# First weight blocks loaded one stage early, store waits moved to the stages that read the data, and a reordered gather stage in a graph-transformer kernel

## What is computed

```
xn = layernorm(x)
x  = x + graph_net(xn, edges) + linear_attention(xn)       # graph_net: x1 = xn @ W1 + b1, then 4 hops
x  = x + mixture_of_experts(layernorm(x))                  # 8 experts, top 2
xn = layernorm(x)
x  = x + (xn @ W.T + bias) + relu_linear_attention(xn)     # W: 1024x1024, scattered from 20000 edge weights
x  = x + gated_mlp(layernorm(x))                           # int32 weights, hidden 384
```

## The kernel before

| tag | function | work |
|---|---|---|
| gs | graph_sort | sorts the edges into buckets (the scatter of the sorted slots runs beside em and m0, on POOL) |
| em | embed | layernorm, x1 = xn @ W1 |
| m (first) | attention, called m0 | q, k, v for 8 head pairs, softly mapped |
| o (first) | project_and_count, o0 | output projection, and the counts and weights of the graph by one-hot products |
| gb, gl | graph_overflow, graph_layer | the 4 hops |
| ro, ex | route, experts | router and scatter to seats; 27 tiles of expert work |
| se | serve | gathers the experts' rows, adds them, layernorm, product with the scattered W |
| m (second) | attention, m1 | as m0, with relu |
| o (second) | project, o1 | output projection, layernorm |
| ff | gated_mlp | last stage |

## Time and profile before

### The profile page before, as it was taken

The page is one execution under the profiler, slowest core; times in us unless marked ns, Lnnn a source line. Parts: engine busy times, 40 slices in busy tenths (PEclk is TensorE's granted clock), DMA queues, the critical chain, the costliest instruction groups (busy, mean ns, idle before and its releaser), DMA issues. The chain is left out here.

```text
span 2633.7 us, 33722 instructions
## 1 busy us (share of the span) xinstructions
PE 2250.2 (85%) x12654; PEld 1997.2 (76%) x12654; DVE 1629.6 (62%) x2675; ACT 1018.6 (39%) x1616; POOL 252.4 (10%) x259
## 2 busy tenths in 40 slices
PE   1689999996994999944499999985979999979798
PEld 1669999995783877744388888874769999978697
DVE  8865555665875788844499999976733333335422
ACT  1512222223863454411488888862111221221120
POOL 0357760000000000002000000002100000000000
PEclk9899999998996999955699999997989999989899
DMA  0251211113442000056545544315421111133314
GB/s 15 83 175 38 66 39 37 42 43 120 131 130 68 9 9 9 20 200 220 199 173 203 183 161 163 142 49 211 159 73 37 52 57 37 48 114 127 119 44 132
DMA packets 104211, 259.04 MB, mean 98 GB/s; under 512 B 17103, under 2 KB 44102, under 8 KB 104046
## 3 DMA queue, kind: packets, MB, share of 16 engines
q1 hardware_dynamic: 93230, 235.88, 25.7%
q0 software_dynamic: 10816, 20.99, 2.8%
HBM read 291.69 MB, written 84.49 MB: 143 GB/s over the span
## 5 line engine op out<-in xcount | busy, mean ns | idle before, releaser
L2050 DVE TENSOR_TENSOR ex_wl<-ex_raw,ex_wh 128x1024 fp32r<-128x1024 f32 x324 | 375.7, 1219 | 58.2 <-ACT ex_wh L2117 57.5
L2117 ACT ACTIVATE ex_wh<-ex_raw 128x1024 fp32r<-128x1024 f32 x324 | 328.8, 1057 | 92.7 <-DMA ex_raw<-in_experts 58.0
L1362 DVE TENSOR_TENSOR m_kvf<-m_bank,m_bkv 128x256 f32<-128x256 f32 (+1 forms) x160 | 67.9, 424 | 232.0 <-PE m_bank L1267 216.1
L1031 POOL DMA_INDIRECT scratch_slots<-pay,idx x160 | 198.4, 1240 | 59.8 <-issue 59.8
L1267 PE MATMUL m_bank<-m_w_lo,xh 128*128 128x256 f32 (+1 forms) x1280 | 178.3, 281 | 0.0
L1267 PE MATMUL m_bank<-m_w_hi,xl 128*128 128x256 f32 (+1 forms) x1280 | 177.4, 280 | 0.2 <-issue 0.2
L1267 PE MATMUL m_bank<-m_w_hi,xh 128*128 128x256 f32 (+1 forms) x1280 | 177.5, 281 | 0.1
L1523 PE MATMUL gl_bank<-gl_gh,gl_al 125*125 125x512 f32 x400 | 158.9, 397 | 8.7 <-DVE gl_al L1691 8.7
L1267 PEld LDWEIGHTS m_bank<-m_w_lo,xh 128*128 128x128 f32 (+1 forms) x1280 | 163.9, 186 | 0.1
L1267 PEld LDWEIGHTS m_bank<-m_w_hi,xl 128*128 128x128 f32 (+1 forms) x1280 | 162.4, 186 | 0.6 <-issue 0.6
L1267 PEld LDWEIGHTS m_bank<-m_w_hi,xh 128*128 128x128 f32 (+1 forms) x1280 | 161.4, 186 | 0.6 <-issue 0.6
(11 more groups left out here) (407 smaller groups left out, 5241.3 us busy)
## 6 DMA issues: line engine op xcount, KB each, us to landing
ex_raw<-in_experts SPq DMA_DIRECT2D x324, 512.0 KB
m_w_raw<-in_qkv SPq DMA_DIRECT2D x48, 512.0 KB
ex_xr<-scratch_seats SPq DMA_DIRECT2D x27, 512.0 KB, 3.7
scratch_served<-ex_y SPq DMA_DIRECT2D x27, 512.0 KB, 2.6
scratch_at<-m_ats SPq DMA_DIRECT2D x48, 209.0 KB, 1.9
o_ar<-scratch_at SPq DMA_DIRECT2D x18, 512.0 KB
o_xr<-scratch_res SPq DMA_DIRECT2D x18, 512.0 KB
scratch_res<-o_xr SPq DMA_DIRECT2D x18, 512.0 KB
```

What stands on the lines that cost most here:

```text
L1031: e.indirect_dma_start(dram["slot_rows"], bass.IndirectOffsetOnAxis(idx[:, k:k + 1].bitcast(U32), 0), pay[:, k, :], None).then_inc(scat.se ...
L1362: e.tensor_tensor(f, bank[KVB + s % 3][0:r, 0:W2], bkv[0:r], ALU.add)
L2050: return e.tensor_tensor(wl[:, n % RING], raw[:, unit[1]], wh[:, n % RING].bitcast(F32), ALU.subtract)
L2117: e.activation(wh[:, n % RING], raw[:, unit[1]], ACT.Copy).then_inc(high.sem)
```

## The change

1. Two buffers now live over all stages: `raw` (four weight slots of 128x1024) and `xr` (three chunks of 128x1024; attention's output staging `ats` is a view of it). `Ahead` loads the first weight units of the next stage into `raw` while the present one still runs: 8 small units in gs for em; 3 in em for m0; 4 in m0 for o0; 4 in ex (at its tile 13) for se; 3 in se for m1; 4 in m1 for o1; 2 in o1 for ff. SP waits, where needed, for the last `make_low` that reads a slot. o1's ring shrinks from 6 slots to 4. Semaphores of such loads are handed on to the next stage.
2. The waits for `res` stores at the end of o0, ro, se and o1, for `at` stores at the end of m0 and m1, and for the `x2` stores at the end of gl are gone; SP of the stage that reads the data waits for them ahead of its loads. em and ex keep theirs.
3. gl's last update is handed to SP chunk by chunk instead of all five at once.
4. o0, se and o1 have new orders on ACT and DVE, below all `serve`: the Sqrt table is loaded at once by a dummy (`warm`), the Sqrt of the first chunk and `scale(0)` come before weight units 2 to 7, `mix(1)` between them, PE turns chunk 1 after the product of chunk 0 instead of within it, the third gather goes ahead of POOL's bias addition.

```diff
+class Ahead:
+    def __init__(self, p, raw, units):
+        self.raw, self.units = raw, units
+        self.loaded = [p.raises(f"ahead{s}", [u], 16) for s, u in enumerate(units)]
+
+    def load(self, e, w_dram, s):
+        e.dma_start(self.raw[:, s], w_dram[self.units[s]]).then_inc(self.loaded[s].sem, 16)
...
 class Resident:
...
     def make_high(self, e, u):
         s = u % self.slots
-        e.wait_ge(*self.loaded[s][u])
+        e.wait_ge(*(self.ahead.loaded if u < self.slots else self.loaded)[s][u])
```

attention, SP at its end:

```diff
+            for s in (3, 0, 1, 2):
+                if s < 3:
+                    e.wait_ge(*low[s][PAIRS - 1])
+                ahead.load(e, then, s)
             store(PAIRS - 1)
-            for t in range(NT):
-                e.wait_ge(*stored[t][PAIRS - 1])
```

project, SP:

```diff
+            for t in at_stored:
+                e.wait_ge(*t.last())
             load_at(0)
-            for u in range(SLOTS):
-                w.load(e, w_dram, u)
             load_at(1)
+            for t in base_stored:
+                e.wait_ge(*t.last())
...
+                if c == 1:
+                    e.wait_ge(*w.low[KC - 1])
+                    for s in range(2):
+                        ahead.load(e, then, s)
```

project, ACT (DVE likewise with make_low, and o0 similarly):

```diff
+            w.make_high(e, 0)
+            w.make_high(e, 1)
             split_at(0)
-            for u in U:
+            for u in range(2, KC):
                 w.make_high(e, u)
```

graph_layer, the end of DVE and of SP:

```diff
-            update(1, range(HALF)).then_inc(last_out.sem)
+            for d in range(HALF):
+                update(1, [d]).then_inc(last_out.sem)
...
+            for c in T[HALF:]:
+                e.wait_ge(*last_out[c])
+                move(e, dram["x2"][nodes(c)], g[:, c], stored[c].sem)
```

experts, SP:

```diff
+                if s == NTILE // 2:
+                    for t in range(4):
+                        ahead.load(e, then, t)
```

serve, ACT:

```diff
+            e.activation(warm[:], share[:, 0, 0:1], ACT.Sqrt)
             w.make_high(e, 0)
             w.make_high(e, 1)
             weigh(0)
-            for u in range(2, 4):
-                w.make_high(e, u)
+            w.make_high(e, 2)
+            w.make_high(e, 3)
+            n.root(e, 0)
+            w.make_high(e, 4)
+            w.make_high(e, 5)
             split(0)
-            for u in range(4, KC):
-                w.make_high(e, u)
+            w.make_high(e, 6)
+            w.make_high(e, 7)
             weigh(1)
```

## The result

The changed kernel takes 2587.0 us (median, 2584.3 to 2587.9) beside 2621.9 for the kernel before: ratio 0.9868, with a 95% interval of 0.9851 to 0.9885. That is 34.9 us gained, where 41.1 were forecast; 2587.0 lies inside the range of 2571 to 2593.

The account below looks back on a forecast made before the run. PE, busy 85% of the span, was taken as the bound, with the winnable idle time at stage changes. Eight terms summed to 41.1 us, taken off the median 2621.5 to give 2580.4 us (bounds 2575 to 2592; 8-in-10 range 2571 to 2593).

Parts of the forecast that it names:

- a new wait of PE of 3 us or more: At any stage's start: a sign that would show the prediction wrong; 3 us or more.
- m0 to o0: Start of o0: barrier behind the `at` landing 1.3, early splits 1.3, unit 7's sooner high part 1.6; 4.2 us.
- gl to ro: End of gl: stores begin 2.7 sooner by chunkwise handover, and the store wait of 2.1 goes to ro; 4.8 us.
- serve: Start of serve: low parts moved 2.3, addition's collision 2.1, xl sooner 5.5, gather sooner 2.0, less 2.3; 9.6 us.
- Rival 2: Ends of o0, se and gl: removed waits sit in the barrier anyway, 7.3 us lost, 2588; chance 0.07.
- Rival 3: Early loads are issued behind an SP wait lasting to the stage's end; 13.7 us lost, 2594; chance 0.05.
- rival 4: In ex: the four early loads meet PE at 99% busy and cost 5.9 us, 2586; chance 0.08.
- (d): Start of serve: chunk 0's gather is faster with 2 MB out of SP's queue; 2.0 us (0 to 3.5).
- the bubble of 2.3: Serve: PE turns chunk 1 behind chunk 0's product, so chunk 1's xh and xl stand open once; 2.3 us lost.
- (b): Start of serve: DVE's one-column multiply no longer collides with POOL's bias addition; 2.1 us (0 to 2.3).
- slack of 2 or more: Chunk 0's product in serve, some 13 us: its slack would hide the moved bias addition's cost of up to 2.5.
- rival 1: Serve's start gives half, 5.5 us: gather bound by its descriptors, addition still collides, weights perhaps late; 2585; chance 0.15.

Follow-up runs that it names:

- the other two unedited serves: waits_back and late_m_ff, which leave serve's start as in the changed kernel; with the changed kernel, se's idle time plus length spans 158.2 to 161.2 us.
- four_first_turn_in: Changed kernel with all four early units split before weigh(0) and mix(0), PE turning chunk 1 within chunk 0's product: 2602.5 us, ratio 0.9857.
- weigh1_early: Changed kernel with weigh(1) ahead of the high parts of units 6 and 7 on ACT: se's idle time plus length 156.7 us.
- waits_back: Changed kernel with the waits for each stage's own stores back at the ends of m0, o0, gl, ro, se, m1 and o1: 2598.1 us.
- late_m_ff: Changed kernel with the first weights of m0, m1 and ff loaded by these stages themselves, behind the barrier: 2599.6 us.
- gather2_late: Changed kernel with the third gather behind POOL's bias addition again, as before the change: se the same within 0.4 us.

## Why the prediction was right, and where it was off

**The direction and the mechanism** were right: the gain is the sum of what stage changes lose, each term has its sign, and se is the term that fell shortest of its value: 5.7 in this profile for 9.6. One cost that every stage change pays stood at nothing without a word: the clearing of the semaphores that are handed on. One of the signs of being wrong was seen, "a new wait of PE of 3 us or more": the 3.92 before unit 6. The others were not: in ex and in serve's steady part nothing got longer (13.1 us a chunk in both profiles).

```
                 forecast   bounds        measured
em to m0           4.2    3.8 to 4.8        3.9
m0 to o0           4.2    2.6 to 4.8        3.1
o0 to the graph    2.6    2.0 to 2.7        2.8
gl to ro           4.8    4.0 to 5.2        4.5
serve              9.6    5 to 12           5.7
se to m1           7.4    6.5 to 8          7.8
m1 to o1           3.6    2 to 4.2          3.9
o1 to ff           4.7    4 to 5            5.2
ex's start          -                      -1.6
program's start     -                      -0.7
```

The measured values are idle time and length against the first profile of before (em to m0 idle time alone), and lengths differ by up to 1.7 with the same code, so that a few tenths to either side are luck. The eight terms add up to 36.9 for 41.1, with the two losses to 34.6; the medians differ by 34.9.

**Terms of the starts.** The runs that put one part back measure them. Early weights for m0, m1 and ff: forecast 13.7, measured 13.5. Removed store waits at o0, m1, ro: 2.6, 2.6, 2.1 forecast on top; before gl the idle time grows by 2.5 when the wait is back, at m1's by 2.5, at ro's by 1.6. Rival 2 is out. For m0 to o0 I took 1.3 for the barrier behind the landing; putting the wait back costs 1.6 at o0 and 1.9 at o1. Rival 3 is out by the first rows of ACT, rival 4 by ex at 497.3 with the loads and 498.3 without.

**The step that failed** is the serve sum, "2.3 + 2.1 + 5.5 + 2.0 - 2.3 = 9.6"; 5.7 came in the profile after, 7.5 and 8.7 in the other two unedited serves. Its pieces up to xl of chunk 0 were, if anything, small (11.9 forecast, 13.2 measured behind the gather): (d) was 3.5, at its upper bound. What failed is the bubble of 2.3, which I took for the only price of the new order. I priced PE's turn, but not who is queued behind mix(1) on DVE. The order shown ahead of the prediction has it: two low parts behind mix(1), mix(1) behind weigh(1), weigh(1) behind two high parts, these behind the last DMAs. It cost 2.4 to 3.9 more, in this profile another 1.5 by the fallen clock, and 0.7 by the later gather. Of the first 2.0 is (b): the bias addition did not go away, it moved. The prediction said so, then took it as hidden by "slack of 2 or more"; it had none, since DVE was already 3.09 late. The rest is the order on ACT (with weigh(1) early PE's idle time before unit 6 is gone altogether, because mix(1) then also passes ahead of the addition).

By its number it is rival 1 that came true, 5.5 for serve and 2585. Two of its conditions held: the addition still collides, and the last weights were late (unit 7 waited for its DMA until 1773.85). The first did not: a gather bound by its own descriptors would not have let mix(0) begin 3.5 sooner behind it. That 2587.0 lies within the range is owed to its width, which took rival 1 in.

On (b) the page "SBUF — State Buffer" of the Trainium skill, section "Who interferes with whom", was the better guide: a DVE instruction with two SBUF inputs and a GpSimd one that reads SBUF keep each other out for a whole instruction. The trace agrees, 3.27 beside 3.17 against 1.23 beside one column; DVE's addition ends at 1780.69, 1.09 behind the end of POOL's, about what it takes alone. I also named the wrong cause for the addition's new place: not the third gather, but its late DMA.

**A cost that was left out.** The barrier got longer. POOL clears a stage's semaphores there by ranges: 12 clears in the whole program before, 48 after. By the code this is because a stage that hands semaphores on, or takes them over, has no unbroken range of them to free. The clears in each profile (count, then ns: shortest, median, longest; then first and last start), and POOL's first instruction of ex, before and after:

```profile
L67 POOLq EVENT_SEMAPHORE_RANGE_CLEAR  x12: 93/185/222, 104.2 to 2633.2; - x12
...
L70 POOLq EVENT_SEMAPHORE_RANGE_CLEAR  x48: 43/47/261, 105.3 to 2585.5; - x48
```

```profile
1268.33 0.20 POOL L133 MEMSET ex_ident<- 128x128 f32 x1 [17.16 <-POOLq L68]
...
1243.78 0.20 POOL L158 MEMSET ex_ident<- 128x128 f32 x1 [18.55 <-POOLq L71]
```

From the first clear (1267.86 and 1242.48) to that instruction it is 0.47 before and 1.30 after. Counted in this way at every stage change, each lost 0.2 to 0.8, 5.2 us together (an estimate from the traces); the measured values in the table above have this cost in them. At serve's start it is the later gather, at ex's 0.8 of the 1.6; most of the rest there is that POOL reaches the end of ro 0.6 later, which no run explains. With the store waits back and with late loads the 48 clears and ex's late start stay. A kernel in which all handed-on semaphores lie at one end of the range was not run, so what it would give back is not shown.

**Smaller misses.** gl to ro gained 3.6 in idle time, not 4.8: ro's PE starts 13.0 behind its first load, 12.2 before. ex's start lost 1.6, in all changed kernels alike (52.5 to 53.0 against 51.2). The program's start lost 0.7, also in all (0.5 to 0.9). Eight more loads stand at SP's start there; a kernel without them wasn't run. The bounds of m0 to o0 don't follow from its pieces, whose lower ones add up to 0.5 and not 2.6; the measured 3.1 lies within either.

**Profile and median.** I took the 13.9 between them as lying outside my rows, and it does: m0 was 424.9 in the profiled execution and 412.8 in the second, whose time was 2621.7. In windows of one head pair, the first of before's first profile with a part of it, the second of the changed kernel:

```profile
302.00:359.30 57.30, 52.84 (x362) 51.09 (x361) 32.51 (x65) 13.84 (x34) 43.80 (x37) 0.95 0.20 44
301.50:308.20 6.70, 4.88 (x15) 4.43 (x16) 4.80 (x8) 1.69 (x3) 5.39 (x5) 0.50 0.13 15
```

```profile
295.00:346.20 51.20, 49.39 (x361) 48.96 (x360) 32.54 (x65) 13.77 (x34) 38.72 (x33) 1.00 0.21 49
```

The granted clock is 0.95 against 1.00, and the pair takes 6 us longer. The mean hides what happens: the clock is 0.50 for 6.8 us, right behind a wait of PE for DVE at the change of head pairs (once more at the end of the pair), and full for the rest:

```profile
300.28 0.39 PE L1276 MATMUL m_bank<-m_kvh,m_kvl 128*128 128x258 f32 x1 [1.86 <-DVE m_kvl L1379]
...
304.19 0.69 PE L1283 MATMUL m_bank<-m_qh,m_ml 128*128 128x418 f32 x1 [1.82 <-DVE m_ml L1388]
```

In before's second profile and in the changed kernel's PE has only the second of these waits, 1.8 to 2.0 us at each change of pairs, and the clock stays full. m0's length goes by the number of such stretches behind its start, 6.8 or 10.2 us each: none in the nine profiles with 411 to 413 us, one at 419.0, two at 424.9 and 427.4, three at 431.9 and 432.0. Against its second profile, m0 of before's first has PE working 6.7 us and standing 5.4 us longer. Why the first wait appears in some executions is open. On one chip, where the kernel before ran in 2637.9, m0 took 419 to 432 in four changed kernels; on the others 411 to 413, but for the first profile of before. So two single profiles must not be compared by their spans.

## What to carry to other kernels

Where stages are parted by a barrier, what a stage needs first (weights, an activation table) can be fetched in the stage ahead, if a buffer outlives the stage; in ex, em and o1 no cost of it was seen, even beside PE at 99%. And a store need only be awaited by who reads it. Here that was worth 13.5 and 10.1 us of 2622, less what the barriers paid for the semaphores that live on: keep these in a range of their own, so that the rest is still cleared at once (not tried here). When such a start gets shorter, write down for each engine what stands behind every instruction that waits: in an order written by hand, an instruction that needs data which is there (weigh(1)) must not stand behind one that waits for a DMA, and moving that one instruction gave 1.5 to 4.5 us. Before two sums of a stage are compared, the granted clock in both has to be looked at: a wait of PE of 2 to 4 us was followed by 3 to 7 us at half speed in some executions and not in others. An operation taken off one place (the bias addition) has to be looked for at its new place.

## What the runs showed of the hardware

The DMA engines are full at the start of serve: a share of 1.00 to 1.03 and 376 to 416 GB/s for 20 us before the change, from 1781 to 1801, and 1.03 and 413 GB/s for 11 us in four_first_turn_in. Issuing two loads 9 us sooner into that brought the first of them 1 us sooner; a load issued at 1778.5 was there for ACT at 1791.3.

PE's granted clock fell to 0.50 for 3.4 us behind an idle time of 3.92 (after), for 3.4 behind one of 2.61 (weigh1_early) and for 6.8 at one of 1.86 with 1.82 soon behind it (m0 in the first profile of before). Behind idle times of 2.37, 2.84 and 3.13 before unit 6 (waits_back, late_m_ff, gather2_late) it stayed full. With the same code at its start, se's sum differs by 3 us and m0's length by up to 20 us between executions, and the clock goes with both.

Where POOL cleared four or five ranges of semaphores at a barrier and not one (o0, ro, ex, m1, o1, ff), the next stage's first instruction came 0.4 to 0.8 us later behind the first clear.
